# Routed experts' down product: from whole-precision matmuls to three passes of rounded parts

## The chip, the cores and the metric

The program runs on one core of one Trainium2 chip. The metric is device time in microseconds for one launch; three runs of the kernel before have the median 1573.19 us (1570.36 to 1573.49). The core's engines are TensorE (PE, with its weight loads shown apart as PEld), VectorE (DVE), ScalarE (ACT), GpSimd (POOL) and SyncE (SP); each works off its own list of instructions in order, and they meet only through semaphores.

## The reference, cut to what matters

Input is 8 x 512 tokens of 512 numbers in float32. A layer norm, an attention block, a residual and a second norm come first. Then a router picks 2 of 16 experts for every token, and for the routed part

```
h1 = einsum('th,ehi->tei', x, w_up)            # 512 -> 256, per expert
a = relu2(h1) * combine[:, :, None]            # square of the positive part, times the weight
routed = einsum('tei,eih->th', a, w_down)      # 256 -> 512, per expert
shared = relu2(x @ shared_up) @ shared_down    # 512 -> 1024 -> 512, for every token
```

The sum of both is normalised and added to the residual. Everything is float32.

## The kernel before, in words

The program has four parts one after the other: attention, the shared expert for the first four batches (`first_order`), the routed experts (`experts_order`), and the shared expert for the last four batches with the combination of all results (`combine_order`). Each part is a list of named steps; every engine walks through the whole list and issues its own instructions for the steps that it knows.

**Routed experts.** The 8192 (token, expert) pairs are sorted by expert into 79 tiles of 128 rows (NTILE = 79, LAST = 78). All 16 experts' weights lie in SBUF, 2048 numbers in each partition per expert (`K.w`, `K.flat`): 1024 of the up weights, then 1024 of the down weights. A small table `K.te` says for every tile where its expert's weights begin. An engine that wants a tile's weights reads that number into a register (`value_load`, in the trace a TENSOR_LOAD with register operations behind it) and addresses by it. For tile i:

- POOL gathers 128 rows of h from HBM (`fetch`, L1801), SP copies them into place with four DMAs (`move`, L1993), DVE transposes them into `hTt` (L1306, semaphore hTt);
- PE `e up` (L827 register load, L829): four float32 matmuls of 256 columns into bank UP, each of which has two records in the trace;
- ACT `e up` (L1639): relu; DVE `e up` (L1314): the square, semaphore e_square;
- PE `e turn2` (L841): two transposes of the square into bank T2; DVE `e turn2` (L1321): the copy `eaT` out of it;
- PE `e down` (L852): two float32 matmuls of 512 columns into bank DN, two records each; ACT `e down` (L1649): copy into one of seven buffers `eyo`; SP `e down` (L1997): store to HBM.

The list staggers the tiles: in step i stand `e turn` of tile i, `e up` of tile i-1, for i under 10 also ACT's DMA of late experts' weights (`late weights`, L577), `e turn2` of tile i-2 and `e down` of tile i-3. Every buffer between engines (UP, T2, DN, hTt, ear, eav, eaT) is double. In the last steps, the list `OVER` adds work for the part behind: SP reloads the shared weights and h, and ACT rounds them (L1578, L1567).

**Three passes.** The attention projections and the shared expert already multiply in another way: each operand is held as a rounded high part (float32r, made by an ACT copy) and a low part (the difference, made by a DVE subtraction), and PE adds high x high, low x high and high x low. One such matmul of 512 columns has one record. The helper is `thrice` (L109 to L114), and the shared expert's own are at L761 and L783.

Of the kernel before, what the change touches and what calls it, by code (L numbers as in the profile page):

```python
# [13 lines left out]
P = 128  # L14
# [31 lines left out]
LAST = NTILE - 1  # L46
LATE = [(e_, n) for e_ in range(E) if GROUP[e_] > 3 for n in range(2)]
KINDS = ("n", "y", "h")


class Box:
# [252 lines left out]
def experts_order():  # L304
    out = []
    for i in range(NTILE + 3):
        if i < NTILE:
            out.append(("e turn", i))
            if i + 7 < NTILE:
                out.append(("fetch", i + 7))  # L310
            if i + 3 < NTILE:
                out.append(("move", i + 3))
        if 0 <= i - 1 < NTILE:
            out.append(("e up", i - 1))
        if i < len(LATE):
            out.append(("late weights", i))
        if 0 <= i - 2 < NTILE:
            out.append(("e turn2", i - 2))
        if 0 <= i - 3 < NTILE:
            out.append(("e down", i - 3))  # L320
        out += OVER.get(i - 3, [])
    return out
# [50 lines left out]
class Sems:  # L373

    def __init__(self, make):
        many = lambda name, n: [make(f"{name}{i}") for i in range(n)]
        self.x0 = many("x0_in", 4)
        self.x, self.ident, self.w1, self.w1b, self.w2, self.w3 = (make(n) for n in (
            "x_in", "ident_in", "w1_in", "w1b_in", "w2_in", "w3_in"))
        self.KR, self.stack = many("KR_in", 2), many("stack_in", RS)  # L380
        self.QR, self.w_hi, self.w_lo = many("QR_in", 2), make("w_high"), make("w_low")
        self.xn_hi, self.c_hi, self.cx_hi, self.cx_lo = make("xn_high"), make("c_high"), make("ctx_high"), make("ctx_low")
        self.x2, self.x1s, self.h2s, self.hTs = make("x2_in"), make("x1_out"), make("h_out"), make("hT_out")
        self.full, self.free = many("ms_full", 2), many("ms_free", 2)
        self.set, self.small, self.sel, self.rope = make("set_done"), make("dve_step"), make("sel_set"), make("rope_done")
        self.var = {k: make(f"var_{k}") for k in KINDS}
        self.off = {k: make(f"off_{k}") for k in KINDS}
        self.root = make("root_step")
        self.dT = make("dT_done")
        self.apart, self.apart_lo, self.plant_hi = (make(n) for n in ("apart_full", "apart_low", "plant_high"))  # L390
        self.scaled = {k: make(f"scaled_{k}") for k in KINDS}
        self.x1, self.hi = make("x1_done"), make("kq_high")
        self.top, self.max = make("top_full"), make("max_done")
        self.score, self.exp, self.acc, self.pv = make("score_full"), make("exp_done"), make("acc_done"), make("pv_done")
        self.kept, self.rden, self.cx = make("ctx_kept"), make("rden_done"), make("ctx_done")
        self.su, self.sd, self.hT = make("su_in"), make("sd_in"), make("hT_in")
        self.su_hi, self.su_lo, self.sd_hi, self.sd_lo = (make(n) for n in ("su_high", "su_low", "sd_high", "sd_low"))
        self.h_hi, self.h_lo = make("h_high"), make("h_low")
        self.up, self.relu, self.aT_hi, self.sq, self.aT_lo = (make(n) for n in ("up_full", "relu_done", "aT_high", "sq_done", "aT_low"))
        self.dn, self.so, self.sos = make("dn_full"), make("so_done"), many("sh_out", 2)  # L400
        self.ew, self.tok, self.cc = many("ew_in", 6), make("tok_in"), make("cc_in")
        self.sig, self.A, self.totals, self.choice = (make(n) for n in ("sig_done", "A_done", "totals_full", "choose_step"))
        self.te, self.prefix, self.slots = make("te_done"), make("prefix_done"), make("slots_done")
        self.pair, self.inv, self.idx = make("pair_done"), make("inv_done"), make("idx_done")
        self.ht, self.hx, self.yps = many("ht_in", 4), many("hx_in", 4), many("yp_out", 7)
        self.hTt, self.eu, self.ear, self.eav, self.eT2, self.eaT, self.ed, self.yo = (make(n) for n in (
            "hTt_done", "eu_full", "e_relu", "e_square", "eT2_full", "eaT_done", "ed_full", "yo_done"))
        self.su2, self.sd2 = many("su2_in", 4), make("sd2_in")
        self.su2_hi, self.sd2_hi = make("su2_high"), make("sd2_high")
        self.cs2 = make("cs2_out")  # L410
        self.cg, self.cin, self.cs = many("cg_in", R), many("cx_in", R), many("cs_out", R)
        self.add, self.cve, self.sqrt, self.coff, self.cn, self.co = (make(n) for n in (
            "add_done", "c_var", "c_sqrt", "c_off", "c_scaled", "c_out"))
# [66 lines left out]
def ffn_room(K, tile):  # L480
    K.su = tile([P, 4, SI])
    K.fhT = tile([P, 2, 4, S])
    K.far = tile([P, 2, S])
    K.fso = tile([P, 2, D])
    K.sd = tile([P, 8, D])
    K.faT = tile([P, 8, S])
    K.w = tile([P, E, WEIGHTS])
    K.te = tile([1, NTILE + 1], I32)
    K.sl1 = tile([P, NT], I32)
    K.sl2 = tile([P, NT], I32)  # L490
    K.g1 = tile([P, NT])
    K.g2 = tile([P, NT])
    K.tok = tile([P, NT])
    K.row = tile([P, P])
    K.count = tile([P, NTILE])
    K.slots = [(tile([P, NT]), tile([P, NT])) for _ in range(2)]
    K.idx = tile([P, NTILE], I32)


def split_room(K, tile):  # L500
# [17 lines left out]
def second_room(K, tile):  # L518
    tile([P, 9 * 4 * S])
    K.su2 = tile([P, 4, SI])  # L520
    K.sd2 = tile([P, 8, D])


def hot_room(K, tile):
# [25 lines left out]
    K.ntv = tile([P, E])  # L550


HOME = (6, 7, 3, 4, 0, 1, 2)


def expert_room(K):
    room = K.fhT[:, 1], K.faT
    K.ht = room[0]
    K.hx = K.fhT[:, 0]
    K.eyo = [K.faT[:, k, :] for k in HOME]  # L560
    K.hTt = K.fso
    K.eaT = K.faT[:, 5, :].rearrange("p (z f) -> p z f", z=2)
    K.eav = K.far[:, :, FI:]
    K.ear = K.far[:, :, 0:FI]
    K.flat = K.w.rearrange("p e n -> p (e n)")
# [14 lines left out]
def tensor_program(e, K, Z):  # L580
# [263 lines left out]
    def e_down(i):  # L844
# [3 lines left out]
            w.wait_ge(Z.yo, i - 1)  # L848
        else:
            w.wait_ge(Z.so, 4 * FIRST)  # L850
        for k in range(2):
            t = e.matmul(K.DN[z][:], K.eaT[:, z, k * P:(k + 1) * P], K.flat[:, bass.ds(reg[i] + 4 * FI + k * D, D)],  # L852
                         start=k == 0, stop=k == 1)
        t.then_inc(Z.ed, 1)

    stages = {"turn": turn, "proj": proj, "v": v, "half": half, "plant": plant, "bias": bias, "top": top, "rows": rows, "scores": scores,
              "values": values, "total": total, "project": project, "turn2": turn2, "route": route, "fold": fold, "up": up,
# [7 lines left out]
def vector_program(e, K, Z):  # L865
# [450 lines left out]
    def e_turn2(i):  # L1316
        z = i % 2
        w.wait_ge(Z.eT2, i + 1)
        if i >= 2:
            w.wait_ge(Z.ed, i - 1)  # L1320
        e.tensor_copy(K.eaT[:, z, :], K.T2[z][:, 0:FI]).then_inc(Z.eaT, 1)  # L1321

    csteps = Steps(Z.add)
    dsteps = Steps(Z.cve)
# [60 lines left out]
    def finish(t):  # L1385
# [4 lines left out]
        if t == NT - 1:  # L1390
            w.wait_ge(Z.add, csteps.n)
            for half in range(2):
# [7 lines left out]
    stages = {"stat": stat, "aggr": aggr, "split w": split_w, "plant low": plant_low, "turn": turn, "low": low, "proj": proj, "half": half, "bias": bias, "top": top, "invert": invert,  # L1400
              "project": project, "fold": fold, "split h": split_h, "split up": split_up, "split down": split_down, "up": up,
              "choose early": lambda n: advance("early", n), "choose late": lambda n: advance("late", n), "invert rows": spread,
              "index": index, "e turn": e_turn, "e up": e_up, "e turn2": e_turn2, "weigh": weigh, "add": add, "rescale": rescale, "finish": finish}
    for name, *at in K.order:
        if name in stages:
            stages[name](*at)
# [2 lines left out]
def scalar_program(e, K, Z, ins):  # L1409
# [174 lines left out]
    def up(b, i):  # L1584
# [4 lines left out]
        if b == FIRST:  # L1589
            w.wait_ge(Z.ed, NTILE)  # L1590
            if i in HOME:
                n7 = HOME.index(i)
                w.wait_ge(Z.yps[n7], 16 * ((LAST - n7) // 7 + 1))
        if n >= 2:
            w.wait_ge(Z.sq, n - 1)
        e.activation(K.ar[:, n % 2, :], K.UP[n % 2][:], ACT.Relu).then_inc(Z.relu, 1)
# [42 lines left out]
        e.activation(K.ear[:, z, :], K.UP[z][:, 0:FI], ACT.Relu).then_inc(Z.ear, 1)  # L1639

    def e_down(i):
        z, r = i % 2, i % 7
        w.wait_ge(Z.ed, i + 1)
        if i >= 7:
            w.wait_ge(Z.yps[r], 16 * (i // 7))
        elif i < 2:
            w.wait_ge(Z.sos[0], 16 * 2 * FIRST)
            w.wait_ge(Z.sos[1], 16 * 2 * FIRST)
        e.copy(K.eyo[r], K.DN[z][:]).then_inc(Z.yo, 1)  # L1649

    def late_weights(n):
        e_, half = LATE[n]
# [21 lines left out]
    def finish(t):  # L1674
        z = PLACE[t] % R
        finished[0] += 1
        if t == NT - 1:
# [7 lines left out]

    stages = {"split w": split_w, "round": round_, "scale": scale, "turn": turn, "proj": proj, "v": v, "half": half, "plant": plant, "repeat": repeat, "rows": rows, "scores": scores, "keep": keep,
              "turn2": turn2, "route": route, "split h": split_h, "split up": split_up, "round up": round_up,
              "round down": round_down, "up": up, "store": store, "choose early": choose, "late weights": late_weights, "e up": e_up,
              "e down": e_down, "take": take, "rescale": rescale, "finish": finish}
    for name, *at in K.order:  # L1690
        if name in stages:
# [3 lines left out]
def gpsimd_program(e, K, Z, ins):  # L1695
# [118 lines left out]
    def gather(n):  # L1814
        t, z = TILES[n], n % R
        w.wait_ge(Z.ed, NTILE)
        for i in range(LAST - 6, LAST + 1):
            w.wait_ge(Z.yps[i % 7], 16 * (i // 7 + 1))
        if n >= R:
            w.wait_ge(Z.cs[z], 16 * (n // R))  # L1820
        e.indirect_dma_start(K.ya[:, z, :], None, K.yp_d, bass.IndirectOffsetOnAxis(K.sl1[:, t:t + 1], 0)).then_inc(Z.cg[z], 16)
# [9 lines left out]
def sync_program(e, K, Z, ins):  # L1831
# [162 lines left out]

    def e_down(i):
        w.wait_ge(Z.yo, i + 1)
        e.dma_start(K.ypv[i], K.eyo[i % 7]).then_inc(Z.yps[i % 7], 16)  # L1997

    def prepare():
        weights(0)  # L2000
# [66 lines left out]
def program(nc, ins, out):  # L2067
# [12 lines left out]
    with ExitStack() as ctx:  # L2080
# [3 lines left out]
        banks = [ctx.enter_context(nc.psum_tensor(f"bank{i}", [P, S], F32)) for i in range(8)]  # L2084
        K.SC, K.MX, K.MS, K.CT = banks[0:2], banks[2:5], banks[5:7], banks[7]
        K.UP, K.DN, K.TR, K.T2 = banks[0:2], banks[2:4], (banks[4], banks[7]), banks[5:7]
        for tag, room in (("f", ffn_room), ("c", split_room), ("g", second_room), ("h", hot_room), ("s", shared_room), ("a", attention_room)):
            with ExitStack() as st:
                room(K, placer(nc, st, tag))
        choose_room(K)  # L2090
# [80 lines left out]
```

## Time and profile before

| | |
|---|---|
| median of three runs | 1573.19 us |
| the profiled execution | 1560.94 us |
| its span | 1559.1 us |
| PE busy | 1494.1 us (96%), 7006 instructions |
| DVE / ACT / POOL busy | 978.7 / 795.9 / 812.2 us |
| PE records of the experts, L829 / L852 | x632, mean 379 ns / x316, mean 593 ns |
| same shared product in three passes, L783 | x768, mean 393 ns |

PE's records overlap: the mean duration of a record is longer than its share of time. How often one begins is read from the starts of neighbouring records. "PEldq", "ACTq" and "SPq" are the engines' sequencers: register loads, register operations and the issuing of DMAs appear there. The time "[... <-X]" behind a row is how long the engine stood idle before it, and who released it.

In the page's 40 slices, each 39 us long, PE stands at nine tenths or more in almost all; in the slices of the routed experts (about the 28th to the 35th), DVE is at 3 tenths and ACT at 2, the lowest of the whole span, and DMA at 7.

### The profile page before, as it was taken

The numbers are of one execution on the slowest core, as the hardware profiler recorded it, in microseconds if no ns is written. First come the engines' busy times: TensorE is split into PE (matmuls) and PEld (weight loads), VectorE is DVE, ScalarE is ACT, GpSimd is POOL, SyncE is SP. The second block draws the span as 40 slices with busy tenths as digits, with TensorE's granted clock in tenths as the row PEclk, the third lists the DMA queues.
The fourth block names the chain that finished last, engine by engine and source line by source line (L and its number), as shares of the span: only waits on it lengthen the run. The fifth ranks groups of instructions, "written<-read, shape, count | busy, mean of one in ns | idle before, by whom it ended". The sixth has DMA issues, their size and how long they took to land.

```text
span 1559.1 us, 21757 instructions
## 1 busy us (share of the span) xinstructions
PE 1494.1 (96%) x7006; PEld 1018.1 (65%) x7006; DVE 978.7 (63%) x1846; ACT 795.9 (51%) x1428; POOL 812.2 (52%) x820
## 2 busy tenths in 40 slices
PE   4899999999999999999999999999999999989998
PEld 2555656756656566566654578777666666668886
DVE  5667767676767676767667446862333333359998
ACT  4655567566575665665647355432222222275554
POOL 4358697777786977778769530003222222143341
PEclk9899999999999999999999999999999999999999
DMA  5749489587595895966954431627977777696773
GB/s 156 102 60 175 59 141 208 75 180 140 97 205 81 145 198 73 185 134 104 237 80 114 135 118 41 226 83 230 313 226 207 221 220 216 203 351 221 232 234 132
DMA packets 162758, 255.53 MB, mean 164 GB/s; under 512 B 20052, under 2 KB 70356, under 8 KB 160596
## 3 DMA queue, kind: packets, MB, share of 16 engines
q1 hardware_dynamic: 143336, 202.62, 57.1%
q0 software_dynamic: 12864, 41.96, 9.4%
q10 hardware_dynamic: 6448, 9.57, 1.8%
q8 instruction: 58, 0.95, 0.3%
q14 instruction: 52, 0.43, 0.1%
HBM read 103.87 MB, written 58.46 MB: 104 GB/s over the span
## 4 chain that ended last, share of the span: by engine, by line
PE 72%; DMA 10%; DVE 7%; POOL 4%; ACT 3%; issue 3%; SPq 1%; DVEq 0%; POOLq 0%; ACTq 0%
PE bank L113 12%; PE bank L761 10%; PE bank L829 8%; PE bank L852 8%; PE bank L783 6%; PE bank L666 6%; PE bank L680 6%; PE bank L699 5%; DMA a<-a 5%; PE bank L688 5%; POOL a L1737 2%; PE bank L708 2%; DMA f<-f 2%; PE bank L841 1%; DMA f<-h_scratch,f 1%
## 5 line engine op out<-in xcount | busy, mean ns | idle before, releaser
L1737 POOL TENSOR_TENSOR a<-a 128x512 f32<-128x512 f32 x384 | 500.3, 1331 | 113.0 <-ACT a L1526 66.8
L1526 ACT ACTIVATE a<-bank 128x512 f32<-128x512 f32 x512 | 296.6, 597 | 254.4 <-PE bank L688 213.4
L981 DVE TENSOR_REDUCE a<-bank 128x1 f32<-128x512 f32 x512 | 321.6, 681 | 76.4 <-PE bank L666 76.0
L113 PE MATMUL bank<-a 128*128 128x512 f32 (+1 forms) x864 | 239.0, 398 | 7.0 <-DVE a L957 4.4
L680 PE MATMUL bank<-a 128*128 128x512 f32 x512 | 217.4, 425 | 4.5 <-ACT a L1526 4.4
L688 PE MATMUL bank<-a 68*128 68x512 f32 x512 | 204.0, 398 | 3.8 <-ACT a L1516 3.7
L113 PEld LDWEIGHTS bank<-a 128*128 128x128 f32 (+1 forms) x864 | 159.4, 187 | 53.2 <-issue 8.6
L1801 POOL DMA_INDIRECT f<-h_scratch,f x79 | 76.1, 964 | 225.3 <-DMA f<-f 204.1
L666 PE MATMUL bank<-a 128*128 128x512 f32 x512 | 178.6, 414 | 10.8 <-DVE a L981 5.1
L783 PE MATMUL bank<-c 128*128 128x512 f32 x768 | 179.8, 393 | 4.6 <-ACT c L1582 2.5
L761 PE MATMUL bank<-c 128*128 128x512 f32 x768 | 177.3, 390 | 1.7 <-ACT c L1567 1.6
L783 PEld LDWEIGHTS bank<-c 128*128 128x128 f32 x768 | 144.7, 189 | 37.1 <-issue 3.7
L761 PEld LDWEIGHTS bank<-c 128*128 128x128 f32 x768 | 143.8, 188 | 34.6 <-issue 4.1
L680 PEld LDWEIGHTS bank<-a 128*128 128x128 f32 x512 | 96.5, 188 | 98.5 <-ACT a L1526 47.7
L829 PEld LDWEIGHTS bank<-f 128*128 128x128 f32 x632 | 119.8, 190 | 51.8 <-issue 39.3
L829 PE MATMUL bank<-f 128*128 x632 | 149.4, 379 | 2.1 <-issue 1.3
L852 PE MATMUL bank<-f 128*128 x316 | 148.5, 593 | 0.0
L1314 DVE TENSOR_TENSOR f<-f 128x256 f32<-128x256 f32 x79 | 33.4, 423 | 176.9 <-ACT f L1639 176.9
L666 PEld LDWEIGHTS bank<-a 128*128 128x128 f32 x512 | 95.3, 190 | 62.5 <-DVE a L981 28.2
L699 PE MATMUL bank<-a 128*32 128x512 f32 x1024 | 134.3, 611 | 0.0
L688 PEld LDWEIGHTS bank<-a 68*128 68x128 f32 x512 | 97.1, 190 | 19.8 <-ACT a L1516 4.8
L1649 ACT COPY f<-bank 128x512 f32<-128x512 f32 x79 | 46.2, 585 | 119.7 <-PE bank L852 119.7
(202 smaller groups left out, 1788.5 us busy)
## 6 DMA issues: line engine op xcount, KB each, us to landing
a<-a SPq DMA_DIRECT2D x262, 256.0 KB, 9.6
f<-f SPq DMA_DIRECT2D x316, 64.0 KB
yp_scratch<-f SPq DMA_DIRECT2D x79, 256.0 KB, 3.5
a<-in_L_attn_x SPq DMA_DIRECT2D x15, 1024.0 KB, 7.7
x_scratch<-a SPq DMA_DIRECT2D x8, 1024.0 KB, 4.5
h_scratch<-a SPq DMA_DIRECT2D x8, 1024.0 KB, 13.3
hT_scratch<-s SPq DMA_DIRECT2D x8, 1024.0 KB, 9.9
c<-hT_scratch SPq DMA_DIRECT2D x8, 1024.0 KB, 7.2
```

The lines of the kernel that those rows point to most:

```text
L113: t = e.matmul(out, a[n], b[n], start=n == 0 and m == 0, stop=n == len(ah) - 1 and m == 2)
L666: e.matmul(MX[n % 3][:], K.Qc[z][:, j, i * P:(i + 1) * P], K.Kc[z][:, j, :], start=True, stop=True).then_inc(Z.top, 1)
L680: e.matmul(SC[n % 2][:], K.Kc[z][:, j, i * P:(i + 1) * P], K.Qc[z][:, j, :], start=True, stop=False)
L688: e.matmul(SC[n % 2][:], K.KR[0:68, b % 2, j, i * P:(i + 1) * P], K.QR[0:68, u % 2, :], start=False, stop=True).then_inc(Z.score, 1)
L699: t = e.matmul(CT[HD * j:HD * j + HD, :], K.v[:, u % VS, i, HD * j:HD * j + HD], K.pt[:, n % NP, :], start=i == 0, stop=i == 3)
L761: t = e.matmul(bank[:], (K.sul if a else K.suh)[:, k, cut], (K.hTl if c else K.hTh)[:, k, :], start=m == 0, stop=m == 11)
L783: t = e.matmul(bank[:], (K.aTl if a else K.aTh)[:, k, cut], (K.sdl if c else K.sdh)[:, k, :], start=m == 0, stop=m == 23)
L829: t = e.matmul(K.UP[z][:, 0:FI], K.hTt[:, z, k * P:(k + 1) * P], K.flat[:, bass.ds(reg[i] + k * FI, FI)], start=k == 0, stop=k == 3)
L852: t = e.matmul(K.DN[z][:], K.eaT[:, z, k * P:(k + 1) * P], K.flat[:, bass.ds(reg[i] + 4 * FI + k * D, D)], start=k == 0, stop=k == 1)
L981: e.tensor_reduce(K.mx[:, i, j:j + 1], K.MX[n % 3][:], AX.X, ALU.max).then_inc(Z.max, 1)
L1526: e.activation(K.pt[:, n % NP, :], K.SC[n % 2][:], ACT.Exp, scale=SCALE).then_inc(Z.exp, 1)
L1737: e.tensor_tensor(K.acc[:, j, :], a, K.pt[:, n % NP, :], ALU.add).then_inc(Z.acc, 1)
```

## The change

The experts' down product is made like the other products, in three passes with `thrice`. Its parts come from four new steps per tile:

- ACT `e split` reads the tile's register and copies the expert's down weights, 128 x 1024, rounded into `edh`; DVE `e split` waits for that (semaphore w_high), reads the register too, and subtracts `edh` from the weights into `edl` (w_low). Both buffers are double.
- ACT `e turn2` copies the transposed square from the bank, rounded, into `eaTh` (eaT_high); DVE `e turn2` now subtracts that from the bank into `eaTl`, where it copied before (eaT_low).
- PE `e down` waits for w_low and eaT_low and issues six matmuls of 512 columns. It addresses no weights by register any more.

For the room, the output buffers `eyo` go from seven to five. The new line numbers: ACT's split L1679 to L1681, its copy L1688, relu L1659, eviction L1669; DVE's square L1328, split L1339 to L1341, low part L1334, transposition L1320; PE up L841 to L843, transposes L855, `thrice` L116.

```diff
@@ experts_order
         if 0 <= i - 2 < NTILE:
-            out.append(("e turn2", i - 2))
+            out += [("e split", i - 2), ("e turn2", i - 2)]
         if 0 <= i - 3 < NTILE:
             out.append(("e down", i - 3))
@@ rooms
+    K.edh = tile([P, 2, 2, D], F32R)
+    K.edl = [tile([P, 2, D], F32R)]
+    K.eaTl = tile([P, 2, FI], F32R)
...
+def part_room(K, tile):
+    tile([P, 29 * S])
+    K.edl.append(tile([P, 2, D], F32R))
+    tile([P, 2 * S])
+    K.eaTh = tile([P, 2, FI], F32R)
...
-HOME = (6, 7, 3, 4, 0, 1, 2)
+HOME = (3, 4, 6, 7, 0)
+OUT = len(HOME)
@@ tensor_program, e_down
-        for k in range(2):
-            t = e.matmul(K.DN[z][:], K.eaT[:, z, k * P:(k + 1) * P], K.flat[:, bass.ds(reg[i] + 4 * FI + k * D, D)],
-                         start=k == 0, stop=k == 1)
-        t.then_inc(Z.ed, 1)
+        w.wait_ge(Z.w_lo, SPLITS + i + 1)
+        act = [[t[:, z, k * P:(k + 1) * P] for k in range(2)] for t in (K.eaTh, K.eaTl)]
+        weight = [[t[:, k, :] for k in range(2)] for t in (K.edh[:, z], K.edl[z])]
+        thrice(e, K.DN[z][:], act, weight).then_inc(Z.ed, 1)
@@ vector_program
     def e_turn2(i):
         z = i % 2
         w.wait_ge(Z.eT2, i + 1)
-        if i >= 2:
-            w.wait_ge(Z.ed, i - 1)
-        e.tensor_copy(K.eaT[:, z, :], K.T2[z][:, 0:FI]).then_inc(Z.eaT, 1)
+        w.wait_ge(Z.eaT_hi, i + 1)
+        e.tensor_tensor(K.eaTl[:, z, :], K.T2[z][:, 0:FI], K.eaTh[:, z, :], ALU.subtract).then_inc(Z.eaT, 1)
+
+    def e_split(i):
+        w.wait_ge(Z.te, 1)
+        w.wait_ge(Z.w_hi, SPLITS + i + 1)
+        at = e.value_load(K.te[0:1, i:i + 1], min_val=0, max_val=(E - 1) * WEIGHTS)
+        given = K.flat[:, bass.ds(at + 4 * FI, 2 * D)].rearrange("p (k n) -> p k n", k=2)
+        e.tensor_tensor(K.edl[i % 2], given, K.edh[:, i % 2], ALU.subtract).then_inc(Z.w_lo, 1)
@@ scalar_program
+    def e_split(i):
+        w.wait_ge(Z.te, 1)
+        for n in range(GROUP[min(i, E - 1)] + 1):
+            w.wait_ge(Z.ew[n], 16 * 2 * GROUP.count(n))
+        if i >= 2:
+            w.wait_ge(Z.ed, i - 1)
+        else:
+            w.wait_ge(Z.dn, 4 * FIRST)
+        at = e.value_load(K.te[0:1, i:i + 1], min_val=0, max_val=(E - 1) * WEIGHTS)
+        given = K.flat[:, bass.ds(at + 4 * FI, 2 * D)].rearrange("p (k n) -> p k n", k=2)
+        e.copy(K.edh[:, i % 2], given).then_inc(Z.w_hi, 1)
+
+    def e_turn2(i):
+        z = i % 2
+        w.wait_ge(Z.eT2, i + 1)
+        if i >= 2:
+            w.wait_ge(Z.ed, i - 1)
+        e.copy(K.eaTh[:, z, :], K.T2[z][:, 0:FI]).then_inc(Z.eaT_hi, 1)
```

ACT's instructions in the routed experts, from one relu to the next but one, before (f and p are SBUF rooms, "bank" is PSUM, a TENSOR_LOAD with ISA rows behind it is a register load):

```order
L1639 ACTIVATE f<-bank 128x256 [waits e_square,eu_full]
L1649 COPY f<-bank 128x512 [waits yp_out3,ed_full]
L1639 ACTIVATE f<-bank 128x256 [waits e_square,eu_full]
L1649 COPY f<-bank 128x512 [waits yp_out4,ed_full]
L1639 ACTIVATE f<-bank 128x256 [waits e_square,eu_full]
```

And the same stretch of ACT after, one tile:

```order
L1659 ACTIVATE f<-bank 128x256 [waits e_square,eu_full]
L1679 TENSOR_LOAD f
L1679 ISA x2
L1681 ISA
L1681 COPY f<-f 128x1024
L1688 CAST p<-bank 128x256 [waits eT2_full]
L1669 COPY f<-bank 128x512 [waits yp_out4,ed_full]
L1659 ACTIVATE f<-bank 128x256 [waits e_square,eu_full]
```

Between the relu of one tile and the eviction of another now stand a register load, the weights' high part and the rounded copy.

DVE in the same stretch before, a tile and its neighbour:

```order
L1306 STREAM_TRANSPOSE f<-f 128x512 [waits eu_full,hx_in2]
L1314 TENSOR_TENSOR f<-f 128x256 [waits e_relu]
L1321 COPY f<-bank 128x256 [waits ed_full,eT2_full]
L1306 STREAM_TRANSPOSE f<-f 128x512 [waits eu_full,hx_in3]
```

DVE after:

```order
L1320 STREAM_TRANSPOSE f<-f 128x512 [waits eu_full,hx_in2]
L1328 TENSOR_TENSOR f<-f 128x256 [waits e_relu]
L1339 TENSOR_LOAD f [waits w_high]
L1339 ISA x2
L1341 ISA
L1341 TENSOR_TENSOR f<-f 128x1024
L1334 TENSOR_TENSOR f<-bank,p 128x256 [waits eaT_high,eT2_full]
L1320 STREAM_TRANSPOSE f<-f 128x512 [waits eu_full,hx_in3]
```

The wait for ACT's high part stands on the register load itself, so the load and its register operations come behind that wait, and the low parts behind them.

## Rows read from the trace of the kernel before

**Rows 1.** Busy time by engine (number of records) in two stretches of the experts

```profile
1077.67:1117.20 39.53, 37.39 (x145) 25.13 (x144) 14.21 (x31) 9.48 (x20) 8.02 (x9) 1.00 1.05 343
1117.20:1362.73 245.53, 245.53 (x939) 164.29 (x938) 92.54 (x201) 64.87 (x134) 60.19 (x63) 1.00 0.75 217
```

**Rows 2.** Groups between 1150 and 1340 us: busy us, mean ns, idle before

```profile
L829 PE MATMUL bank<-f 128*128 x416 | 98.3, 379 | 0.0
L852 PE MATMUL bank<-f 128*128 x208 | 98.0, 593 | 0.0
L1306 DVE STREAM_TRANSPOSE f<-f 128x512 f32<-128x512 f32 x52 | 36.5, 702 | 0.0
...
L1649 ACT COPY f<-bank 128x512 f32<-128x512 f32 x52 | 30.4, 585 | 80.8 <-PE bank L852 80.8
```

**Rows 3.** One step in order of time: start us, length us, engine, line

```profile
1183.19 1.89 PE L829 MATMUL bank<-f 128*128 x8
...
1184.92 0.38 PE L841 MATMUL bank<-ident,f 128*128 128x128 f32 x2
...
1185.12 0.38 ACT L1639 ACTIVATE f<-bank 128x256 f32<-128x256 f32 x1 [1.14 <-PE bank L829]
1185.14 1.88 PE L852 MATMUL bank<-f 128*128 x4
1185.53 0.42 DVE L1314 TENSOR_TENSOR f<-f 128x256 f32<-128x256 f32 x1 [2.29 <-ACT f L1639]
...
1185.88 0.42 DVE L1321 COPY f<-bank 128x256 f32<-128x256 f32 x1
...
1186.86 1.89 PE L829 MATMUL bank<-f 128*128 x8
```

**Rows 4.** Where PE waits for a transposition, and line L827 over the span

```profile
1107.37 0.71 DVE L1306 STREAM_TRANSPOSE f<-f 128x512 f32<-128x512 f32 x1 [3.56 <-DMA f<-f]
...
1108.86 1.59 PEld L829 LDWEIGHTS bank<-f 128*128 128x128 f32 x8 [1.68 <-issue]
...
L827 PEldq TENSOR_LOAD <-f x79: 297/307/1200, 1073.8 to 1359.2; - x79
L827 PEldq FUSED_REGOPS  x79: 151/151/165, 1075.1 to 1359.5; - x79
```

**Rows 5.** ACT with its sequencer: a relu and the DMA issue behind it

```profile
1091.46 0.38 ACT L1639 ACTIVATE f<-bank 128x256 f32<-128x256 f32 x1 [1.14 <-PE bank L829]
1091.46 0.37 ACTq L577 DMA_DIRECT2D f<-in_L_ffn_w_down  x1
```

**Rows 6.** Three-pass matmuls (min/median/max ns, first and last start), and wide copies and subtractions

```profile
L783 PE MATMUL bank<-c x96: 389/389/389, 1055.9 to 1077.4; 128*128 128x512 f32 x96
...
L906 DVE TENSOR_TENSOR a<-s,a 128x1280 fp32r<-128x1280 f32 x1 | 1.5, 1492 | 4.6 <-ACT a L1436 4.6
...
L1436 ACT CAST a<-s 128x1280 fp32r<-128x1280 f32 x1 | 1.3, 1257 | 10.5 <-DMA s<-in_L_attn_W_QR 10.5
...
L1290 DVE TENSOR_TENSOR h<-f 128x1024 f16<-128x1024 f32 x8 | 9.7, 1218 | 0.0
```

**Rows 7.** SP's issues behind one another, in order of time

```profile
1120.90 2.53 SPq L1993 DMA_DIRECT2D f<-f  x4
...
1124.16 2.52 SPq L1993 DMA_DIRECT2D f<-f  x4
```

**Rows 8.** The first tiles in order of time: relu of tile 1, down of tile 0

```profile
1081.32 0.38 ACT L1639 ACTIVATE f<-bank 128x256 f32<-128x256 f32 x1 [1.34 <-PE bank L829]
...
1084.15 1.88 PE L852 MATMUL bank<-f 128*128 x4
```

**Rows 9.** The end: up of tile 78, ACT's roundings, the shared expert

```profile
1362.73 1.89 PE L829 MATMUL bank<-f 128*128 x8
...
1367.08 2.18 ACT L1578 CAST c<-g 128x512 fp32r<-128x512 f32 x4
...
1371.83 22.89 PE L761 MATMUL bank<-c 128*128 128x512 f32 x96 [1.61 <-ACT c L1567]
```

More of the change, by code:

```diff
@@ L48 @@
 KINDS = ("n", "y", "h")
+SPLITS = 4
 class Box:
@@ L404, in __init__ @@
         self.pair, self.inv, self.idx = make("pair_done"), make("inv_done"), make("idx_done")
-        self.ht, self.hx, self.yps = many("ht_in", 4), many("hx_in", 4), many("yp_out", 7)
+        self.ht, self.hx, self.yps = many("ht_in", 4), many("hx_in", 4), many("yp_out", OUT)
         self.hTt, self.eu, self.ear, self.eav, self.eT2, self.eaT, self.ed, self.yo = (make(n) for n in (
-            "hTt_done", "eu_full", "e_relu", "e_square", "eT2_full", "eaT_done", "ed_full", "yo_done"))
+            "hTt_done", "eu_full", "e_relu", "e_square", "eT2_full", "eaT_low", "ed_full", "yo_done"))
+        self.eaT_hi = make("eaT_high")
         self.su2, self.sd2 = many("su2_in", 4), make("sd2_in")
@@ L561, in expert_room @@
     K.hTt = K.fso
-    K.eaT = K.faT[:, 5, :].rearrange("p (z f) -> p z f", z=2)
     K.eav = K.far[:, :, FI:]
@@ L1402, in vector_program @@
               "choose early": lambda n: advance("early", n), "choose late": lambda n: advance("late", n), "invert rows": spread,
-              "index": index, "e turn": e_turn, "e up": e_up, "e turn2": e_turn2, "weigh": weigh, "add": add, "rescale": rescale, "finish": finish}
+              "index": index, "e turn": e_turn, "e split": e_split, "e up": e_up, "e turn2": e_turn2, "weigh": weigh, "add": add, "rescale": rescale, "finish": finish}
     for name, *at in K.order:
@@ L1591, in up @@
             if i in HOME:
-                n7 = HOME.index(i)
-                w.wait_ge(Z.yps[n7], 16 * ((LAST - n7) // 7 + 1))
+                home = HOME.index(i)
+                w.wait_ge(Z.yps[home], 16 * ((LAST - home) // OUT + 1))
         if n >= 2:
@@ L1641, in e_down @@
     def e_down(i):
-        z, r = i % 2, i % 7
+        z, r = i % 2, i % OUT
         w.wait_ge(Z.ed, i + 1)
-        if i >= 7:
-            w.wait_ge(Z.yps[r], 16 * (i // 7))
+        if i >= OUT:
+            w.wait_ge(Z.yps[r], 16 * (i // OUT))
         elif i < 2:
@@ L1687, in scalar_program @@
               "turn2": turn2, "route": route, "split h": split_h, "split up": split_up, "round up": round_up,
-              "round down": round_down, "up": up, "store": store, "choose early": choose, "late weights": late_weights, "e up": e_up,
+              "round down": round_down, "up": up, "store": store, "choose early": choose, "late weights": late_weights, "e up": e_up, "e split": e_split, "e turn2": e_turn2,
               "e down": e_down, "take": take, "rescale": rescale, "finish": finish}
@@ L1816, in gather @@
         w.wait_ge(Z.ed, NTILE)
-        for i in range(LAST - 6, LAST + 1):
-            w.wait_ge(Z.yps[i % 7], 16 * (i // 7 + 1))
+        for i in range(LAST - OUT + 1, LAST + 1):
+            w.wait_ge(Z.yps[i % OUT], 16 * (i // OUT + 1))
         if n >= R:
@@ L1996, in e_down @@
         w.wait_ge(Z.yo, i + 1)
-        e.dma_start(K.ypv[i], K.eyo[i % 7]).then_inc(Z.yps[i % 7], 16)
+        e.dma_start(K.ypv[i], K.eyo[i % OUT]).then_inc(Z.yps[i % OUT], 16)
     def prepare():
@@ L2086, in program @@
         K.UP, K.DN, K.TR, K.T2 = banks[0:2], banks[2:4], (banks[4], banks[7]), banks[5:7]
-        for tag, room in (("f", ffn_room), ("c", split_room), ("g", second_room), ("h", hot_room), ("s", shared_room), ("a", attention_room)):
+        for tag, room in (("f", ffn_room), ("c", split_room), ("g", second_room), ("p", part_room), ("h", hot_room), ("s", shared_room), ("a", attention_room)):
             with ExitStack() as st:
```

## The prediction, made before the changed kernel ran

> **What bounds the kernel now.** I read the page first: PE is busy 96% of the span, so the question is what it does and whether it ever waits. Then I cut the span into stretches. The busy time by engine in the routed experts shows PE at 245.53 of 245.53 us from 1117.20 to 1362.73, clock 1.00, while DVE has 92.54 us and ACT 64.87 [rows 1]. PE has 14 records to a tile (8 + 2 + 4), so 939 of them are 67 tiles, and a tile takes 3.665 us. The timeline of one step says the same: up starts at 1183.19 and again at 1186.86. Inside, the up product takes 1184.92 - 1183.19 = 1.73, the two transposes 0.22, the down product 1186.86 - 1185.14 = 1.72 us [rows 3]. The groups confirm that neither PE line has idle time before it, while ACT's eviction sits 80.8 us waiting for PE [rows 2]. So PE's work alone sets this stage; before 1117.20 it also waits for rows (37.39 busy of 39.53 us) [rows 1].
>
> **What is removed: 0.36 us of PE per tile.** The down product goes. In its place come six one-record matmuls of 512 columns. The shared expert shows their pace: 96 from 1055.9 to 1077.4, which is 21.5 over 95 gaps, 0.227 us each, so six take 1.36 us [rows 6]. PE's own work would be 1.73 + 0.22 + 1.36 = 3.31 us a tile. If nothing else mattered, 67 tiles would give back 67 x 0.355 = 23.8 us.
>
> **What is added.** Per tile, ACT gets the weights' high part and the rounded copy, DVE the low part; DVE's copy becomes a subtraction of the same size.
> - ACT, 128 x 1024: between 383 ns for 256 columns (0.38) [rows 3] and 1257 for 1280 [rows 6], so 0.85 ns a column and 1.04 us. The rounded 256-column copy is 0.39.
> - DVE, 128 x 1024: 1.218 us for that size with another output type, 1.492 for 1280 columns of the same kind [rows 6]. I take 1.22; the upper end is 1.49. The 256-column subtraction is taken as 0.42, like the square.
> - A register load on each. Where PE waited for a transposition, that ended at 1107.37 + 0.71 = 1108.08, and the first weight load began at 1108.86: 0.78 us, of which 0.04 is the semaphore (as between L829's end at 1185.08 and the relu at 1185.12) and 0.74 the load with its register operations; the load record alone is 0.30, the first operation 0.15 [rows 3, 4]. Its cost on ACT or DVE is not in this trace. The ends are 0.30 (the load record alone) and 1.20 (the longest one). I take 0.74, the one place where the whole string of instructions could be timed.
>
> As totals these fit: ACT has 0.38 + 1.04 + 0.39 + 0.59 = 2.40, DVE 0.70 + 0.42 + 1.22 + 0.42 = 2.76 us a tile, both under 3.31. SP, back to back, takes 3.26 us a tile (1120.90 to 1124.16) [rows 7], just under too. **The totals are not what decides; the order is.**
>
> **The path through a tile.** ACT's high part of tile k stands behind its relu of tile k+1. PE's down of tile k stands behind up and transposes of tile k+2. From the end of up k+1 to the down of k the new path is: semaphore 0.04; register load on ACT 0.74, begun when the relu is let go; high part 1.04; semaphore 0.04; register load on DVE 0.74, which stands behind the wait; low part of the weights 1.22; low part of the activations 0.42, less 0.08 because neighbours on DVE overlap (1185.88 against 1185.53 + 0.42) [rows 3]; semaphore 0.05. Sum 4.21 us. In the meantime PE has transposes 0.22, down k-1 1.36, up k+2 1.73 and transposes 0.22, less the 0.16 by which up's records outlast its issue: 3.37 us. So PE stands 0.84 us, and 0.10 for the first weight load that is no longer hidden: 0.94. The next up is thereby late, which gives tile k+1 its time, so the stall falls on every second tile. As a cycle over two tiles: 4.21 + 0.10 + 1.36 + up to its visible end 1.89 = 7.56, or **3.78 us a tile** against 3.665. In this stage 67 x 0.115 = **+7.7 us**.
>
> That the load begins with the relu and not before is the pivotal reading. ACT's issue of a DMA behind a relu begins at 1091.46, exactly when the relu does, after 1.14 us of waiting, though nothing held the DMA itself [rows 5]. So ACT's sequencer does not pass an instruction that waits. Half of the load (0.38 us) then runs beside the relu, the rest is on the path. The Trainium skill says otherwise, in Perfetto Trace Analysis, DVE / Act Engine Instruction: an instruction is pushed into a wait queue, and the sequencer is then ready to decode the next. By that rule ACT's load would run ahead of the waiting relu and cost nothing; the row disagrees for a DMA issue, and no row here shows a register load on ACT. The time that this would give is the first rival's.
>
> **The ends of the stage.** At the start, relu of tile 1 at 1081.32 is followed by ACT's DMA issue of 0.42, then 0.74 + 1.04, then on DVE 0.04 + 0.74 + 1.22 + 0.34: 1085.86, so down of tile 0 starts at 1086.0 instead of 1084.15 [rows 8]. In the first ten steps that DMA issue, 0.37 us, is on the path as well and adds 0.19 a tile [rows 5]. Up of tile 3 comes 1.5 us late, and eight tiles at 3.97 instead of 3.665 add 2.4; the 2.14 us that PE waits there now (39.53 - 37.39) [rows 1] take 2.1 of that: **+1.8 us** at 1117.2. At the end, from the start of up of tile 78: relu at 1.93, ACT's split of tile 77 until 3.71, copy until 4.10, eviction of tile 76 until 4.68; then the four roundings for the next part, 2.18 us, stand in front of the split of tile 78 [rows 9], which ends at 7.9; DVE needs 2.34 more, and the last down ends at 11.75. Now the shared expert starts 1371.83 - 1362.73 = 9.10 after that up, and its first 96 matmuls take 22.89 instead of 21.8 because their inputs trickle in [rows 9], 10.2 in all: **+1.6 us**.
>
> **Costed at nothing.** Five output buffers instead of seven: a store is issued at once behind the eviction and 5 x 3.8 us pass before the buffer is wanted. The two further waits on PE's down are for signals already counted. Fewer register operations on PE are hidden there anyway. DMA has the same transfers and a share of 0.75 [rows 1]; the pace of SP stays under the new one.
>
> **Sum:** 7.7 + 1.8 + 1.6 = +11.1 us. Against its own execution, 1560.94 becomes 1572.0 (span 1559.1 to 1570.2). The median of the runs shown is 12.3 us above that execution, and I carry the difference onto the median: 1573.2 + 11.1 = **1584 us**. The break-even is near: 0.23 us less in a cycle of 7.56 and the stage is where it was.
>
> **Rivals.**
> 1. *ACT's register load costs nothing* (it runs ahead of the relu). The high part starts when the relu is through, 0.42 us sooner; the cycle is 7.14, 3.57 a tile: 67 x -0.095 = -6.4, start 0, end +1: about 1568 us. For it: the skill's rule above. Against it: the DMA issue [rows 5].
> 2. *PE stays the bound.* Loads on ACT and DVE near the lower end: 0.30 on each gives 4.21 - 0.88 = 3.33 us of path under PE's 3.37, so 3.31 a tile and -23 us, 1550. SP's 3.26 [rows 7] would let that pass. For it: the totals, and the load record's 0.30. Against it: 0.74 measured in full on PE, twice the record and more, since register operations stand behind the load in the new lists too.
> 3. *Much slower:* ACT's load begins only when the relu has ended, or the loads are dearer there. The place is the same path; 0.38 more in a cycle is 3.97 a tile, 67 x 0.305 = +20 and +5 at the ends: 1598. From 0.23 us below my sum the change loses, and all above it is loss. For it: the longest load took 1.20 [rows 4]. Against it: the DMA issue that began with the relu, not after it.
>
> **Chances.** Forecast (3.70 to 3.88 a tile) 0.64; rival 1 0.14; rival 2 0.11; rival 3 0.11. A measurement of this kernel can tell about 0.2%, 3 us, from nothing. Faster: 0.11 + 0.12 + 0.01 = 0.24; within: 0.05 of the forecast, 0.02 of rival 1, 0.07; slower 0.69. The range reaches down to rival 1 and up to rival 3 and leaves rival 2 out: 1565 to 1600. The forecast's own is 1578 to 1592, which is what an error of 0.2 us in the cycle makes; DVE's upper end of 1.49 for the split is inside (0.27 more in the cycle, +9 us).
>
> **What the new profile would show.** PE's step in the middle of the experts alternates between about 3.3 and 4.2 us, the idle time sits before the first matmul of L116, and DVE's L1334 releases it. DVE's L1341 starts 0.78 us after ACT's L1681 ends, and ACT's L1681 starts 0.74 after L1659 starts. PE's clock stays at 1.00. PE's busy share of the stage falls from 100% to about 88%. I am wrong if L116 shows no idle time, if L1681 begins right at the end of the relu (rival 1), or if the step is the same for all tiles at 3.3 (rival 2).

## The result, and the profile after

The changed kernel takes 1589.28 us (median of five runs, 1588.99 to 1592.48) against 1570.73 for the kernel before (five runs): 18.6 us slower. The ratio on record is 1.0127, interval 1.0111 to 1.0142; the two medians alone give 1.0118. Forecast were 1584 us and 11 us slower, with 1565 to 1600 as range.

The first trace of the changed kernel has a span of 1586.9 us, 28 more than that of before, which is more than the medians differ by. So each kernel was traced once more, with spans of 1558.1 and 1576.1 us. These two traces are of two chips, on which the medians of the kernel before are 1562.9 and 1561.9 us, so they differ by the change and by little else that is known. They are compared by stages here; the columns are the stretch, its length, then the busy time and number of records of PE, PEld, DVE, ACT and POOL, the granted clock, DMA share and GB/s. The kernel before, second trace:

```profile
1076.52:1117.59 41.07, 37.67 (x145) 25.05 (x144) 15.06 (x32) 9.50 (x20) 8.56 (x9) 1.00 1.05 332
1117.59:1363.09 245.50, 245.50 (x939) 164.29 (x938) 91.84 (x201) 65.01 (x134) 59.08 (x62) 1.00 0.75 217
1363.09:1371.31 8.22, 7.48 (x25) 3.98 (x24) 1.29 (x4) 4.87 (x10) 0.00 (x0) 1.00 0.99 335
1371.31:1558.10 186.79, 176.12 (x768) 143.77 (x768) 157.21 (x402) 106.29 (x203) 69.20 (x64) 0.99 0.71 232
```

The changed kernel, second trace, cut at the same events (first up, up of tile 11, up of tile 78, first matmul of the shared expert, end):

```profile
1076.19:1118.73 42.54, 36.06 (x164) 28.44 (x163) 24.07 (x39) 22.13 (x40) 9.04 (x9) 1.00 1.06 334
1118.73:1380.00 261.27, 238.97 (x1074) 187.25 (x1073) 167.90 (x268) 150.02 (x269) 60.95 (x62) 1.00 0.68 201
1380.00:1391.35 11.35, 7.11 (x32) 5.33 (x32) 6.66 (x10) 9.66 (x18) 0.00 (x0) 1.00 1.02 369
1391.35:1576.10 184.75, 175.12 (x769) 143.66 (x767) 155.97 (x400) 104.15 (x199) 65.95 (x64) 0.99 0.69 228
```

The difference of 18.0 us is +1.5 in the first tiles, **+15.8 in the 67 steps between tiles 11 and 78**, +3.1 at the end of the stage, -2.0 in the part behind it, and -0.3 ahead. Between the two first traces the 67 steps differ by 16.5 us, the first tiles by 3.1 and the end of the stage by 3.5: the middle is firm to 1 us, the first tiles are so only to 1.6. A step went from 3.664 to 3.900 us (3.910 in the first trace). PE, which had no idle time in the middle [rows 1], is now busy 239 of 261 us. It has less to do and waits more.

The groups of the first trace between 1150 and 1340 us, which answer to [rows 2] and [rows 3]:

```profile
L116 PE MATMUL bank<-f,p 128*128 128x512 f32 x148 | 59.4, 429 | 16.1 <-DVE f L1334 15.8
L1681 ACT CAST f<-f 128x1024 fp32r x49 | 51.4, 1048 | 24.5 <-issue 24.5
...
L1341 DVE TENSOR_TENSOR f<-f 128x1024 fp32r<-128x1024 f32 x25 | 30.6, 1225 | 37.0 <-ACT f L1681 30.5 <-issue 6.4
...
L1334 DVE TENSOR_TENSOR f<-bank,p 128x256 fp32r<-128x256 f32 x49 | 20.4, 417 | 0.0
```

PE's only idle time stands before L116, and DVE's L1334 ends it. Ahead of ACT's split stands "issue": the engine waits for nothing but its own sequencer. What that is the chain shows, here over one cycle of two tiles, from an end of L1334 to the next on the chain (start us, length us, what):

```profile
1201.84 1.67 PE bank L116 x6
1203.51 1.80 PE bank L843 x8
1205.31 0.02 issue
1205.33 0.35 ACT f L1659
1205.68 0.03 issue
1205.70 0.15 ACTq L1679
...
1206.02 1.06 ACT f L1681
1207.08 0.03 issue
1207.11 0.30 DVEq L1339
1207.41 0.03 issue
1207.44 0.19 DVEq L1339
...
1208.97 0.43 DVE f L1334
```

Down, up, relu, register load on ACT, high part, register load on DVE, low parts, down again: the path of the prediction, step for step. (The register load in this piece is one of the short ones: from the relu's start to ACT's split it is 1206.02 - 1205.33 = 0.69 us, where the mean is 0.9.)

### The profile page after: what moved, and what is told of

It is laid out like the page before. It is cut to its first block, busy times and chain, and to the rows that moved or that the text cites. A ratio compares the mean times of both kernels' runs of the same rounds, so it can differ in the third digit from the quotient of the medians.

```text
span 1586.9 us, 22790 instructions
## 1 busy us (share of the span) xinstructions
PE 1492.5 (94%) x7164; PEld 1049.2 (66%) x7164; DVE 1067.5 (67%) x1925; ACT 895.9 (56%) x1586; POOL 815.3 (51%) x820
## 4 chain that ended last, share of the span: by engine, by line
PE 66%; DVE 8%; issue 7%; ACT 6%; DMA 6%; POOL 4%; DVEq 2%; ACTq 1%; SPq 1%; another core or an unknown queue 0%; POOLq 0%
PE bank L116 16%; PE bank L775 10%; PE bank L797 8%; PE bank L680 6%; PE bank L694 6%; PE bank L713 5%; DMA a<-a 5%; PE bank L702 5%; PE bank L843 4%; POOL a L1776 2%; ACT f L1681 2%; PE bank L722 2%; DVEq L1339 1%; DVE f L1334 1%; PE bank L618 1%
## 5 line engine op out<-in xcount | busy, mean ns | idle before, releaser
L116 PE MATMUL bank<-a 128*128 128x512 f32 (+1 forms) x864 | 240.3, 400 | 7.0 <-DVE a L971 4.4
L116 PEld LDWEIGHTS bank<-a 128*128 128x128 f32 (+1 forms) x864 | 160.3, 188 | 53.2 <-issue 8.6
L843 PE MATMUL bank<-f 128*128 x632 | 150.9, 382 | 1.3 <-issue 1.2
L843 PEld LDWEIGHTS bank<-f 128*128 128x128 f32 x632 | 116.0, 189 | 26.8 <-issue 8.7
L116 PE MATMUL bank<-f,p 128*128 128x512 f32 x238 | 96.6, 433 | 30.7 <-DVE f L1334 30.3
L1681 ACT CAST f<-f 128x1024 fp32r x79 | 82.8, 1048 | 40.8 <-issue 40.8
L1063 DVE TENSOR_TENSOR c<-c 128x512 fp32r<-128x512 f32 x64 | 44.4, 695 | 79.5 <-ACT c L1625 66.9
```

The source lines that it names most:

```text
L116: t = e.matmul(out, a[n], b[n], start=n == 0 and m == 0, stop=n == len(ah) - 1 and m == 2)
L843: t = e.matmul(K.UP[z][:, 0:FI], K.hTt[:, z, k * P:(k + 1) * P], K.flat[:, bass.ds(reg[i] + k * FI, FI)], start=k == 0, stop=k == 3)
L1681: e.copy(K.edh[:, i % 2], given).then_inc(Z.w_hi, 1)
```

## The experiments

Each is an edit of the changed kernel; the last two rows are the two kernels as they are. All compute what the changed kernel computes, except where the expectation names what is left out. "Step" is the mean between the first up matmuls of tiles 11 and 78. The column "before" is the median of the kernel before on the same chip, and the ratios are to runs there; three chips were used, so times are compared between rows with the same number in that column, and otherwise by ratio. A step is read from one trace each.

| run | step | time us | before us | ratio (interval) |
|---|---|---|---|---|
| DVE's load ahead of its wait | 3.604 | 1566.24 | 1570.31 | 0.9987 (0.9970 to 1.0004) |
| ACT's load ahead of the relu | 3.617 | 1564.97 | 1570.31 | 0.9978 (0.9958 to 0.9999) |
| both | 3.419 | 1544.68 | 1570.31 | 0.9871 (0.9822 to 0.9920) |
| weights' parts made once | 3.393 | 1544.6, one run | 1570.31 | |
| split ahead of up in the list | 3.383 | 1543.45 | 1562.93 | 0.9875 (0.9850 to 0.9899) |
| both loads, store on POOL | 3.382 | 1545.27 | 1562.93 | 0.9891 (0.9864 to 0.9918) |
| parts waited for, whole product | 4.042 | 1592.47, one run | 1562.93 | |
| split ahead, roundings later | 3.379 | 1545.02 | 1561.91 | 0.9896 (0.9868 to 0.9924) |
| DVE's load twice | 4.187 | 1610.57, one run | 1561.91 | |
| the changed kernel again | 3.900 | 1578.28, one run | 1561.91 | |
| the kernel before again | 3.664 | 1559.89, one run | 1562.93 | |

**DVE's register load ahead of its wait.**

```diff
         w.wait_ge(Z.te, 1)
-        w.wait_ge(Z.w_hi, SPLITS + i + 1)
         at = e.value_load(K.te[0:1, i:i + 1], min_val=0, max_val=(E - 1) * WEIGHTS)
+        w.wait_ge(Z.w_hi, SPLITS + i + 1)
```

> DVE's register load is issued before its wait for ACT's high part, not behind it; nothing else changes. Theory (the path through a tile sets the step): of the 0.77 us between DVE's load and its split only one register operation stays behind the wait, about 0.15; the cycle over two tiles shrinks from 7.82 to 7.20 us, the step from 3.91 to 3.60, and with the ends the time falls by about 23 us, to 1566. Rival (occupancy: ACT, DVE or SP are simply too full, or PE's six passes are dearer than thought): the instructions are the same ones, so the step stays at 3.91 and the time at 1589.

The step is 3.604, the time 1566.2: as the path has it. The same instructions in another order are worth 23 us (22 by the ratios, 1.0127 and 0.9987), and the occupancy rival falls.

**ACT's register load ahead of the relu.**

```diff
+    def address(i):
+        w.wait_ge(Z.te, 1)
+        where[i] = e.value_load(K.te[0:1, i:i + 1], min_val=0, max_val=(E - 1) * WEIGHTS)
...
     def e_up(i):
         z = i % 2
+        if i:
+            address(i - 1)
         w.wait_ge(Z.eu, i + 1)
...
```

> ACT's register load is issued ahead of the relu that it stood behind; nothing else changes. Theory of the path: ACT's split begins when the relu is through, 0.32 us after its start instead of 0.885, so the cycle is 7.82 - 0.565 = 7.25, the step 3.63, the time about 1569. Rival (occupancy): step 3.91, 1589. Second rival (ACT's sequencer runs past the waiting relu anyway and the 0.885 us are something else, such as ACT's own recovery): no change, and the gap between relu and split stays.

Step 3.617 and 1565.0 us, where 3.63 and 1569 were expected. The second rival falls too: the load did stand behind the relu, and moving it pays.

**Both.**

> Both register loads are taken off the path. Theory: the cycle would be 7.82 - 0.62 - 0.565 = 6.63 us, 3.32 a tile, which is PE's own work; the two gains add up (or end at 3.32), the time falls by 67 x 0.59 = 39 and some 4 at the ends, to about 1546, faster than the kernel before (1570.7). Rival (occupancy of DVE, ACT or the supply of rows by SP at 3.26 us a tile plus its hiccups): the step ends at 3.45 or above and the time above 1555.

1544.7 us, ratio 0.9871: 26 us faster than before by the medians, 20 by the ratio. In the timeline, ACT's split now begins 0.28 us after the relu's start, and DVE's 0.15 us after ACT's end (1203.07 + 1.04 = 1204.11):

```profile
1202.79 0.39 ACT L1667 ACTIVATE f<-bank 128x256 f32<-128x256 f32 x1 [1.39 <-PE bank L843]
...
1203.07 1.04 ACT L1690 CAST f<-f 128x1024 fp32r x1
...
1204.26 1.22 DVE L1341 TENSOR_TENSOR p<-f 128x1024 fp32r<-128x1024 f32 x1 [0.62 <-issue]
```

PE is busy 228.46 of the 229.05 us of the 67 steps:

```profile
1115.22:1344.27 229.05, 228.46 (x1073) 186.43 (x1074) 173.93 (x268) 145.53 (x268) 69.76 (x63) 1.00 0.79 230
```

The step is 3.42 and not 3.32, so something small is left. PE's own register load is part of it, the one for the up weights that the kernel before had too:

```profile
L841 PEldq TENSOR_LOAD <-f x67: 296/411/958, 1116.9 to 1343.2; - x67
```

It begins 0.04 us after DVE's transposition ends, and up begins 0.44 to 0.60 us after it. Over the 67 steps the time above 3.341 us a tile (the median of the next run) is 5.2 us; 2.8 of that stand in the 26 steps where this load took over 0.5 us, 0.9 in four steps where rows came late.

**Weights' parts made once.**

```diff
-            out += [("e split", i - 2), ("e turn2", i - 2)]
+            out += [("e split", i - 2)] * (i < 4) + [("e turn2", i - 2)]
...
-        w.wait_ge(Z.w_lo, SPLITS + i + 1)
+        w.wait_ge(Z.w_lo, SPLITS + min(i, 1) + 1)
```

> The high and low parts of the down weights are made for tiles 0 and 1 only and used for all later ones; the product is thus with the wrong weights, all other work is as in the changed kernel. It shows the floor: the six matmuls with the activations' parts alone. Theory: PE-bound, 3.31 to 3.35 us a tile, L116 without idle time, the experts' stage about 269 us long instead of 317. Rival (the six passes cost more than 1.36 us, or rows come too slowly): above 3.45.

The mean step is 3.393, the median 3.341: PE's own work is near the 3.31 that was forecast. Most of what the mean lies above the median stands in rows that come late: 2.8 of 3.5 us are in eleven steps whose up stood directly behind a transposition that had waited for its rows. DVE's transposition waits for the row DMAs 33 times, 43.4 us of DVE's time in all:

```profile
L1320 DVE STREAM_TRANSPOSE f<-f x66: 696/711/715, 1120.3 to 1339.9; 128x512 f32<-128x512 f32 x66
...
  DMA f<-f: 43.4, 33
```

With both loads off the path, the kernel is thus within 0.03 us a tile of having no weights' splits at all (one trace each).

**Split ahead of up in the list**, loads as in the changed kernel.

```diff
+        if 0 <= i - 2 < NTILE:
+            out.append(("e split", i - 2))
         if 0 <= i - 1 < NTILE:
             out.append(("e up", i - 1))
...
-            out += [("e split", i - 2), ("e turn2", i - 2)]
+            out.append(("e turn2", i - 2))
```

> Only the place in the list changes: the split of tile i-2 now stands before up of tile i-1 (on ACT before the relu, on DVE before the square), with both register loads as in the changed kernel. Theory of the path: ACT's split no longer waits for up of the next tile, the path from down k-2 to down k is under PE's own work, and the step falls from 3.91 to the floor of 3.39 to 3.42 seen with the weights' parts made once; the time about 1545 to 1549. Rival (the loads cost in themselves, wherever they stand, since every engine has more to do): the step stays above 3.6 and the time above 1560.

Step 3.383, 1543.45 us, ratio 0.9875. The register loads are all there and cost nothing, because ACT's split no longer stands behind the relu of the next tile. The cause is the order, with the loads as the size of it. This version and the one with both loads moved, with what is built on each, are the ones that beat both kernels.

**Both loads, output stored by POOL** (SP's step `e down` moved to POOL's program, unchanged).

> Both register loads off the path as in the run before last, and the output tiles are stored by POOL instead of SP. Theory (the floor of 3.42 us a tile is the supply of rows: SP needs 3.26 us for four copies and a store, back to back, and loses its lead with every hiccup): without the store SP needs 2.6 us, DVE's transposition no longer waits for rows, the step falls to 3.33 and the time by about 6 us, to 1539. Rival (the floor is the DMA engines' or PE's own, and POOL's store is dearer than SP's): no change, or slower, 1544 or more.

Half right. No transposition waits for rows any more, and the step falls from 3.419 to 3.382, its median to 3.342. What is left above that median is therefore not the supply of rows; 2.0 of the 2.7 us stand in 17 steps where PE's register load took over 0.5 us. But the first eleven tiles take 40.7 us instead of 38.9, and the time gains nothing (0.9891 against 0.9871, intervals that overlap).

**Parts waited for, whole product.**

```diff
-        thrice(e, K.DN[z][:], act, weight).then_inc(Z.ed, 1)
+        whole = [K.eaTh[:, z, k * P:(k + 1) * P].bitcast(F32) for k in range(2)]
+        for k in range(2):
+            t = e.matmul(K.DN[z][:], whole[k], K.flat[:, bass.ds(reg[i] + 4 * FI + k * D, D)], start=k == 0, stop=k == 1)
+        t.then_inc(Z.ed, 1)
```

> All parts are made and waited for as in the changed kernel, but PE multiplies in whole precision as before, from the rounded activations and the weights in SBUF. Theory: PE's work returns to 3.665 a tile, the cycle becomes 7.82 + 0.36 = 8.18, so 4.09 a tile, and the time about 1589 + 67 x 0.18 = 1601: the three passes by themselves are worth 12 us even here. Rival (PE-bound after all, the passes being the cost): the step returns to 3.67 and the time to 1571.

Step 4.042 (expected 4.09), and 1592.5 us against 1578.3 for the changed kernel again: 14 us above it, 12 were expected. These are single runs on two chips, whose medians of before are 1 us apart. The three passes do save PE's time; half of the 0.36 us would be 0.18 in the step, 0.14 was measured (4.042 against 3.900).

**Split ahead, roundings later.**

```diff
-OVER = {LAST - 5: [("reload up",)], LAST - 3: [("reload h",), ("reload down",)], LAST - 2: [("round up", i) for i in range(4)],
-        LAST - 1: [("split h", FIRST, k) for k in range(4)] + [("round up", 4), ("round up", 5)], LAST: [("round up", 6), ("round up", 7)]}
+OVER = {LAST - 5: [("reload up",)], LAST - 3: [("reload h",), ("reload down",)],
+        LAST - 1: [("split h", FIRST, k) for k in range(4)] + [("round up", i) for i in range(6)], LAST: [("round up", 6), ("round up", 7)]}
...
```

> On top of the split placed before up (the version with 1543): the four roundings of the shared weights that ACT does between its eviction of tile 76 and its split of tile 78 (2.2 us) move behind the eviction of tile 77. Theory: they stand in front of the last tile's split, so the last down and with it the shared expert begin up to 2.2 us sooner: 8.8 to 9.5 us after up of tile 78 instead of 11.0, and the time falls by 1 to 2 us, which is at the edge of what three rounds tell. Rival (the shared expert then waits for the roundings or for h instead): the same time, the wait stands at the shared up product.

Against the version with the split ahead alone, the shared expert begins 9.8 us after up of tile 78 instead of 11.0, but its first 96 matmuls then take 24.2 instead of 21.6 us, waiting for ACT. No gain (1545.0 us, intervals of the ratios that overlap): the rival was right.

**DVE's load twice.**

```diff
         w.wait_ge(Z.w_hi, SPLITS + i + 1)
+        e.value_load(K.te[0:1, i:i + 1], min_val=0, max_val=(E - 1) * WEIGHTS)
         at = e.value_load(K.te[0:1, i:i + 1], min_val=0, max_val=(E - 1) * WEIGHTS)
```

> The changed kernel with DVE's register load done twice behind the wait for ACT's high part. Theory of the path: the second load with its own register operations adds about 0.64 us to a cycle of two tiles, so the step goes from 3.91 to 4.23, the time up by 67 x 0.32 and some 3 at the start, 24 us or so, to about 1613. Rival (the step is set by occupancy, SP or PE): DVE has 0.6 us of slack in a step of 3.91, so nothing changes, 1589.

Step 4.187, +0.287 against the changed kernel's 3.900; expected was +0.32. The second load lengthens the way from ACT's high part to DVE's split from 0.81 to 1.44 us, 0.63 more; the way from the relu to ACT's split is 0.06 shorter than in the changed kernel, and half of the remaining 0.57 is 0.287. A cost put on DVE's sequencer appears in the step by half, as a cycle over two tiles has it. The time rose by 32 us, more than the expected 24: 67 x 0.287 = 19.2, 4.8 in the first eleven tiles, 3.5 at the end, and 4.9 ahead of the experts, where this edit does nothing and which stays unexplained (the trace with ACT's load moved has as much there, 1081.7 against 1076.2 us).

**The two kernels again.**

> The kernel before, unchanged, for a second trace of it: its first trace, 1560.94, was some 10 us under its own median. If the difference lies in the attention part or in the clock of the last part, the experts' stage (294.2 us from the first up to the shared expert) is the same within 1 us; if it lies in the experts, that part is longer.

> The changed kernel itself once more, for a second trace on the chip of these runs: the mean step between tiles 11 and 78 should again be 3.9 us and the stage from the first up to the shared expert 316 to 318 us; the part behind it, 191.5 us in the first trace against 187.3 before, tells whether those 4 us belong to the change (then 191 again) or to that one execution (then 185 to 188).

The stage of before is 294.8 us (294.2 in the first trace), and the part behind it 186.8 (187.3): its two traces agree. Beside the second one the median is 1562.9, 10 us under that of the first runs; where those 10 us lie no trace shows, since both traces are of short executions. In the changed kernel the stage is 315.2 us (317.2 in the first trace), and the part behind it 184.75, not 191.5: the 4 us there do not belong to the change. Over all traces that part, whose instructions are the same, takes 184.8 to 192.2 us.

## Why the prediction was right, and which term was too small

**What bounds, and where it went.** Right: PE's work set the stage, and the change replaced it by a path. The stall stands before the first matmul of L116 and DVE's L1334 ends it, as was said. The size was short: +7.7 us were given for the 67 steps, +15.8 were measured. The time, 1589.3 us, is within the forecast's own 1578 to 1592, partly because the median that 11.1 us were added to (1573.2) was higher than that of the five runs (1570.7): of the loss itself 11.1 of 18.6 us were forecast. PE's busy share of the 67 steps fell to about 92%, where 88 was forecast.

**The cycle.** The term that was sized too small is ACT's register load. Means over the 46 of 63 tiles at which PE's down came late, first trace, in us:

| part of the cycle | forecast | measured |
|---|---|---|
| relu's start to ACT's split (register load) | 0.74 | 0.92 |
| ACT's high part | 1.04 | 1.05 |
| to DVE's split (semaphore, register load) | 0.78 | 0.80 |
| DVE, both low parts | 1.56 | 1.56 |
| to L116, and L116 to the next up | 1.51 | 1.56 |
| up to the next relu | 1.93 | 1.95 |
| sum | 7.56 | 7.84 |

Half of 7.84 is 3.92, the measured step 3.91. Of the 0.28 us that the sum lacked, 0.18 are this term and the rest is spread over the others. The 0.74 us had been timed on PE, where the load record takes 0.307 us in the median [rows 4]. On ACT behind the relu it takes 0.497 in this trace, up to 1.02, and 0.449 in the second (min/median/max ns):

```profile
L1679 ACTq TENSOR_LOAD <-f x79: 272/497/1024, 1082.3 to 1386.5; - x79
```

and ahead of the relu, in the experiment, it takes 0.284:

```profile
L1658 ACTq TENSOR_LOAD <-f x79: 273/284/726, 1084.3 to 1367.0; - x79
```

The prediction had named 0.30 and 1.20 as its ends and took the middle by PE. The old step of 3.665 is 7.33 us in a cycle, 0.23 under the forecast sum, and that 0.23 was the loss that was given; an error of 0.28 more than doubled it. The 0.10 us for the first weight load had no row behind it; from the first down matmul to the next up 1.46 were given and 1.51 measured.

**The pivotal reading held.** ACT's register load began 5 to 7 ns after the start of the relu before it, in all 67 steps of both traces, never ahead of it. That is what the DMA issue had shown [rows 5]. The Trainium skill's rule of the wait queue (Perfetto Trace Analysis, DVE / Act Engine Instruction), after which the sequencer goes on to decode behind a waiting instruction, did not give the time here: what stands behind a waiting relu does not start until the relu is let go.

**The stall's pattern** was off. Forecast was 0.94 us on every second tile; measured 0.63 on 46 of 63. The delay is not all on one of two neighbours, and steps range from 3.38 to 4.32 (tenth and ninetieth percentile). The mean hangs on the cycle's sum alone.

**The ends.** By the second traces they were sized right: at the start +1.5 against +1.8 forecast; in the last stretch +3.1, less 1.6 that the first 96 shared matmuls win back (21.6 against 23.2 us), so +1.5 against +1.6. By the first traces they are +3.1 and +3.0 (3.5, less 0.5 won back), so the agreement is partly luck. The four roundings do stand in front of the last split; PE then idles 2.1 us twice.

**Rivals.** The first (ACT's load costs nothing) is what the experiment with the load ahead of the relu makes true, and the second (PE stays the bound) what the one with the split ahead of up does: 5 us under before by the medians where 5 were given, and 19 where 23 were. In the changed kernel itself neither held. The third, dearer loads on ACT, is in part what happened: 0.18 of its 0.38 us. That five output buffers cost nothing is borne out: with the split ahead they are still five, and the step is 3.383.

**PE's saving** was sized right: six matmuls and the rest are 3.34 us a tile where nothing waits, 3.31 were forecast.

## What to carry to other kernels

Taking work from the engine that bounds pays only if the parts that the new form needs are ready without it: add up the path from one product to the next that depends on it, over as many tiles as the buffers are deep, and compare that sum with the engine's own time, before the engines' totals. A register load behind a wait was 0.8 us of path on DVE and 0.9 on ACT here; issue it ahead of the wait. And of two steps in one engine's list the one that has its inputs already goes first: here that alone turned 18 us lost into 19 us gained.

## What the runs showed of the hardware

- **The time of a register load varies, by place and within one place.** The TENSOR_LOAD took 0.28 us in the median on ACT beside an eviction, and 0.50 beside the relu (0.45 in the second trace); on DVE 0.31 behind the wait, 0.38 ahead of it, where DVE was mostly at work; on PE 0.31 in the kernel before and 0.41, up to 0.96, with both loads moved. With the output stored by POOL, ACT's took 0.58 in the 67 steps beside the same eviction: 0.70 where the end of one of SP's DMA issues fell into the load and 0.29 where not. In the changed kernel the same comparison gives 0.54 and 0.40. A longer load is also likelier to have such an end in it, so this does not show that the issuing of DMAs slows it; what does stays open.
- **The clock at the end of the stage.** In the first trace of the changed kernel, after PE had idled 2.26 us in front of one down product, the granted clock fell from 1.00 to 0.54, near the level of 1.2 GHz, in the next stretch, and matmul records went from 0.39 to 0.63 us. The second trace has nearly the same idle time (2.12 us, twice) and no fall. With both loads moved PE idled 1.50 and 2.02 us there and the clock of the next 7 us was 0.76; with the split ahead it idled 3.27 us and the clock stayed at 1.00. So such a gap can cost the clock, but does not always, and its length alone does not tell. The two stretches of the first trace:

```profile
1383.00:1389.50 6.50, 4.24 (x21) 3.35 (x21) 3.55 (x5) 4.84 (x10) 0.00 (x0) 1.00 0.96 352
1389.50:1397.00 7.50, 6.06 (x16) 4.28 (x15) 3.96 (x6) 6.13 (x12) 0.00 (x0) 0.54 0.93 338
```
